# Softmax sums taken from the first pass of the scores by ScalarE, in place of a second product by TensorE

## The reference

```python
x_ln = layernorm(x, ln_g, ln_b)                  # transposed, and read again as (b, 1024, 256)
q = x_flat @ wq + bq
o = gelu(depthwise_conv7x7(q as image, stride 2) + dw_b)
offsets = conv1x1(o, pw_w)                       # 2 numbers at each of 16 x 16 places
interp = bilinear samples of x at refs + tanh(offsets)          # 256 rows of 256 channels
v = interp @ wv + bv ;  k = interp @ wv + bv
qh, kh, vh = heads(q @ mq_w + mq_b), heads(k @ mk_w + mk_b), heads(v @ mv_w + mv_b)
attn = softmax(qh @ kh^T, axis=-1)               # 1024 x 256 for each of 8 heads
z = (attn @ vh, heads joined) @ mo_w + mo_b + x
out = gelu(layernorm(z) @ mlp_w + mlp_b) + z
```

## Time and profile before

| | |
|---|---|
| median of 3 runs | 514.39 us (514.14 to 515.91) |
| profiled execution | 512.36 us |
| span of its trace | 510.6 us |
| TensorE matmul busy | 454.9 us, 89% |
| TensorE weight load busy (overlaps) | 318.8 us, 62% |
| VectorE busy | 286.2 us, 56% |
| ScalarE busy | 211.6 us, 41% |
| GpSimd (POOL) busy | 120.1 us, 24% |
| mean granted TensorE clock | 0.98 |

### The profile page before, as it was taken

One profiled execution on the slowest core, in us unless ns is written; L12 is line 12 of the kernel. 1 busy time (PEld: TensorE's weight loads), 2 busy tenths in 40 slices (PEclk: granted clock), 3 DMA queues, 4 the chain that ended last, 5 costly groups with the idle time before them and its releaser, 6 DMA issues.

```text
span 510.6 us, 9319 instructions
## 1 busy us (share of the span) xinstructions
PE 454.9 (89%) x3743; PEld 318.8 (62%) x3743; DVE 286.2 (56%) x609; ACT 211.6 (41%) x338; POOL 120.1 (24%) x163
## 2 busy tenths in 40 slices
PE   6788979988989999989899999989899897888956
PEld 5657756645567576656686666656767564665735
DVE  4518446846673367667754345567546647625433
ACT  1122212545346045655333336745173664662230
POOL 5420301167003001681002003761030030100000
PEclk9999989989999999999999999999999998999978
DMA  7298866581947930293157801472226200000202
GB/s 211 76 168 171 163 101 126 85 169 65 137 69 99 233 54 3 85 124 64 42 101 103 164 3 46 90 111 27 83 42 86 83 3 2 1 2 2 82 2 83
DMA packets 30489, 42.90 MB, mean 84 GB/s; under 512 B 6075, under 2 KB 21230, under 8 KB 30446
## 3 DMA queue, kind: packets, MB, share of 16 engines
q1 hardware_dynamic: 23598, 34.82, 37.4%
q0 software_dynamic: 3584, 4.50, 3.8%
q10 hardware_dynamic: 3264, 2.99, 2.9%
HBM read 16.16 MB, written 4.19 MB: 40 GB/s over the span
## 4 chain that ended last, share of the span: by engine, by line
PE 57%; DVE 13%; DMA 10%; POOL 7%; issue 5%; ACT 5%; SPq 1%; ACTq 0%; DVEq 0%; POOLq 0%
PE ps_d L759 8%; PE ps_d L884 5%; PE ps_d L861 5%; PE ps_d L961 5%; PE ps_d L747 4%; PE ps_s L808 4%; DMA xa<-in_x_dram 4%; PE ps_v L850 4%; DMA corners<-in_x_dram,row_of 3%; PE ps_v L844 3%; PE ps_t L827 3%; PE ps_d L779 3%; POOL samp L1937 3%; DVE mx L1613 3%; PE ps_d L903 2%
## 5 line engine op out<-in xcount | busy, mean ns | idle before, releaser
L1226 ACT ACTIVATE prob<-ps_t 128x1024 f32<-128x1024 f32 x64 | 65.4, 1021 | 95.8 <-PE ps_t L827 92.2
L1613 DVE TENSOR_REDUCE mx<-ps_s 128x4 f32<-128x1024 f32 x64 | 78.2, 1222 | 24.1 <-PE ps_s L808 23.2
L1909 POOL DMA_DIRECT2D q_st<-mx_t x64 | 34.0, 532 | 244.0 <-ACT mx_t L1218 226.0
L759 PE MATMUL ps_d<-cstack,conv_w 128*32 128x256 f32 x1024 | 59.0, 380 | 3.4 <-issue 1.8
L808 PE MATMUL ps_s<-k_st,q_st 96*128 96x256 f32 x256 | 49.9, 317 | 8.2 <-DVE mx L1613 7.1
L759 PEld LDWEIGHTS ps_d<-cstack,conv_w 128*32 128x32 f32 x1024 | 36.3, 108 | 23.9 <-issue 6.2
L808 PEld LDWEIGHTS ps_s<-k_st,q_st 96*128 96x128 f32 x256 | 35.9, 191 | 20.5 <-DVE mx L1613 12.6
L827 PE MATMUL ps_t<-q_st,k_st 98*128 98x256 f32 x256 | 42.6, 289 | 6.2 <-ACT zt L1285 3.0
L827 PEld LDWEIGHTS ps_t<-q_st,k_st 98*128 98x128 f32 x256 | 35.5, 192 | 8.9 <-issue 5.1
L1627 DVE TENSOR_TENSOR att<-ps_v,rden 128x256 f32<-128x256 f32 x32 | 13.6, 424 | 43.2 <-ACT rden L1237 43.2
L844 PE MATMUL ps_v<-prob,vh 128*32 128x256 f32 x512 | 35.1, 392 | 1.5 <-DVE att L1627 1.5
(11 more groups left out here) (178 smaller groups left out, 744.7 us busy)
## 6 DMA issues: line engine op xcount, KB each, us to landing
q_st<-q_parts SPq DMA_DIRECT2D x42, 256.0 KB, 5.6
xa<-in_x_dram SPq DMA_DIRECT2D x8, 512.0 KB, 9.6
z_all<-in_x_dram SPq DMA_DIRECT2D x8, 512.0 KB, 7.9
out_dram<-z_all SPq DMA_DIRECT2D x8, 512.0 KB, 2.6
cstack<-qpad SPq DMA_DIRECT2D x22, 180.5 KB, 5.7
k_st<-cstack SPq DMA_DIRECT2D x22, 128.0 KB, 4.2
q_st<-z_all SPq DMA_DIRECT2D x6, 256.0 KB, 5.7
cstack<-att SPq DMA_DIRECT2D x6, 180.5 KB, 9.8
```

Of the source, the lines that this page charges most:

```text
L759: ins = pe.matmul(ps[32 * k:32 * k + 32, 0, :], conv_w[:, cb * 4 + k, y, x, :], cstack[:, cb, k, y:y + HG_, x:x + WG_], start=n == 0, stop ...
L1226: drain(act.activation(prob[:, u % 2, 2 * pr:2 * pr + 2].rearrange("p h m s -> p (h m) s"), ps_t[:], ACT.Exp), t_ring, "t", b, u, pr)
L1613: drain(dve.tensor_reduce(mx[:, u % 2, half, :], ps_s[:], AX.X, ALU.max), s_ring, "s", b, u, half)
```

## The change

ScalarE takes the sums of a row over the scores of the first pass. VectorE writes the negated maxima of two heads at a time (`max_neg`). ScalarE then takes, for each of the 4 heads, exp(score - maximum) over `ps_s` in place, with the sum of the row as an additional output (`exp_sums`), and this drains `ps_s`. Then it takes the logarithm of the unit's 16 columns of sums (`log_sums`), and VectorE subtracts the negated maxima from it (`maxima_and_sums`), so that `mx` holds maximum + ln(sum). The rest of the way is the same (turning, copy, rest, two DMAs), but the second pass now gives normalised probabilities. `values_summed`, `denominators` and the product with the reciprocal go; VectorE copies the result (`mixed`).

The order changes too: on TensorE `max_rows` stands behind `values`, and in slot 6 the product "g" and `scores1(m, 0)` stand behind `keys`. ScalarE has `exp_sums` of the first half ahead of `max_out` and the first `exps` (except in slot 0), and `exp_sums` of the second half and `log_sums` ahead of the second `exps`. VectorE has `maxima_and_sums` and `mixed` behind the first half's maxima and ahead of `maxima_lo`. 

```diff
@@ dense_order
+        if in_front(b, s, "off"):
+            order += [("off", n)]
+        if in_front(b, s, "qh1") and b:
+            order += [("qh", n, 1, hg) for hg in range(NHG)]
         if unit_of(b, s, 1):
             order += [("mxt", *unit_of(b, s, 1))]
...
-            order += [("tp", m, 1), ("g", m, 1)] * post
+            order += [("tp", m, 1)] * post
...
             order += [("kh", n)]
+        if s == 6:
+            order += [("g", m, 1)] * post
@@ TensorE
             def max_rows(b, u):
                 ps = open_bank(dense, "mxt", b, u)
-                read_by(s_ring, "s", b, u, 1)
+                pe.wait_ge(shift_done.sem, shift_done.at(b, u + 1))
...
-            def values_summed(b, u):
-                for mt in range(2):
-                    for h in range(HQ):
-                        ins = pe.matmul(ps_v[32 * h:32 * h + 32, 1, :], ones[:], prob[:, u % 2, h, mt, :],
-                                        start=mt == 0, stop=mt == 1)
...
             def slot(b, s):
-                if unit_of(b, s, 1):
-                    max_rows(*unit_of(b, s, 1))
...
                 if unit_of(b, s, 3):
-                    values_mixed(*unit_of(b, s, 3))
+                    values(*unit_of(b, s, 3))
+                if unit_of(b, s, 1):
+                    max_rows(*unit_of(b, s, 1))
...
                 if s == 6 and post:
                     project1(m, "tp", w_tp, 1)
-                    project1(m, "g", w_g, 1)
...
-                if unit_of(b, s, 3):
-                    values_summed(*unit_of(b, s, 3))
...
-                if s == 6 and post:
-                    scores1(m, 0)
                 if in_front(b, s, "kh"):
                     keys(n)
                 if s == 6 and post:
+                    scores1(m, 0)
+                    project1(m, "g", w_g, 1)
                     scores1(m, 1)
@@ ScalarE
-            def denominators(b, u):
...
+            def exp_sums(b, u, half):
+
+                with_exp()
+                for h in range(HQ):
+                    if h % 2 == 0:
+                        act.wait_ge(maxed.sem, maxed.at(b, 4 * u + 2 * half + h // 2 + 1))
+                    ins = act.activation(ps_s[:, h, :], ps_s[:, h, :], ACT.Exp, bias=max_neg[:, u % 2, half, h:h + 1],
+                                         accum_out=sums[:, u % 2, half, h:h + 1])
+                drain(ins, s_ring, "s", b, u, half)
+
+            def log_sums(b, u):
+                k = s_ring.use("s", b, u, 1)
+                act.wait_ge(k.drained, k.done)
+                act.activation(sums[:, u % 2], sums[:, u % 2], ACT.Ln).then_inc(sums_log.sem, 1)
...
             def slot(b, s):
-                if unit_of(b, s, 1):
-                    max_out(*unit_of(b, s, 1))
...
+                if s and cur:
+                    exp_sums(b, s, 0)
+                if s and unit_of(b, s, 1):
+                    max_out(*unit_of(b, s, 1))
                 if unit_of(b, s, 2):
                     exps(*unit_of(b, s, 2), 0)
+                if s == 0 and unit_of(b, s, 1):
+                    max_out(*unit_of(b, s, 1))
...
+                if s == 0 and cur:
+                    exp_sums(b, s, 0)
+                if cur:
+                    exp_sums(b, s, 1)
+                    log_sums(b, s)
                 if unit_of(b, s, 2):
                     exps(*unit_of(b, s, 2), 1)
-                if unit_of(b, s, 3):
-                    denominators(*unit_of(b, s, 3))
@@ VectorE
             def maxima(b, u, half):
                 await_bank(dve, s_ring, "s", b, u, half)
...
-                drain(dve.tensor_reduce(mx[:, u % 2, half, :], ps_s[:], AX.X, ALU.max), s_ring, "s", b, u, half)
+                for pr in range(2):
+                    dve.tensor_reduce(max_neg[:, u % 2, half, 2 * pr:2 * pr + 2], ps_s[:, 2 * pr:2 * pr + 2], AX.X,
+                                      ALU.max, negate=True).then_inc(maxed.sem, 1)
+
+            def maxima_and_sums(b, u):
+
+                dve.wait_ge(sums_log.sem, sums_log.at(b, u + 1))
...
+                dve.tensor_tensor(mx[:, u % 2], sums[:, u % 2], max_neg[:, u % 2], ALU.subtract).then_inc(shift_done.sem, 1)
...
-                drain(dve.tensor_tensor(att[:, hg, c0:c0 + S_], ps_v[:, 0, :], rden[:], ALU.mult), v_ring, "v", b, u)
+                drain(dve.tensor_scalar(att[:, hg, c0:c0 + S_], ps_v[:, 0, :], 1.0, None, ALU.mult), v_ring, "v", b, u)
...
             def slot(b, s):
-                if unit_of(b, s, 1):
-                    maxima_lo(*unit_of(b, s, 1))
...
                 if s and cur:
                     maxima(b, s, 0)
+                if unit_of(b, s, 1):
+                    maxima_and_sums(*unit_of(b, s, 1))
+                if unit_of(b, s, 3):
+                    mixed(*unit_of(b, s, 3))
+                if unit_of(b, s, 1):
+                    maxima_lo(*unit_of(b, s, 1))
```

More of the change, by code:

```diff
@@ L140, in dense_order @@
             order += [("vh", b)]
-        if in_front(b, s, "off"):
-            order += [("off", n)]
         if s == 0:
@@ L162, in dense_order @@
         if s == 6:
-            order += [("tp", m, 1), ("g", m, 1)] * post
+            order += [("tp", m, 1)] * post
         if s == 7 and b == 0:
             order += [("z", b, 0, jp) for jp in range(2)]
-        if in_front(b, s, "qh1"):
+        if in_front(b, s, "qh1") and b == 0:
             order += [("qh", n, 1, hg) for hg in range(NHG)]
@@ L294, in build @@
         vh = sb("vh", [P, 2, C])
+        max_neg = sb("max_neg", [P, 2, 2, HQ])
+        sums = sb("sums", [P, 2, 2, HQ])
         mx = sb("mx", [P, 2, 2, HQ])
@@ L297, in build @@
         prob = sb("prob", [P, 2, HQ, 2, S_])
-        rden = sb("rden", [P, S_])
         att = sb("att", [P, NHG, HW])
@@ L386, in build @@
         max_in = [signal(f"max_in{k}", UNITS, 16) for k in range(2)]
-        den_log = signal("den_log", UNITS)
-        rden_done = signal("rden_done", UNITS)
+        maxed = signal("maxed", 4 * UNITS)
+        sums_log = signal("sums_log", UNITS)
+        shift_done = signal("shift_done", UNITS)
         ln2_stat = signal("ln2_stat", NT)
@@ L831, in values @@
             def values(b, u):
-                values_mixed(b, u)
-                values_summed(b, u)
-            def values_mixed(b, u):
                 hg, _ = unit_at(u)
@@ L843, in values_mixed @@
                         hh = hg * HQ + h
[L844 to L851 removed]
+                        ins = pe.matmul(ps_v[32 * h:32 * h + 32, 0, :], vh[:, mt, hh * HD:(hh + 1) * HD],
+                                        prob[:, u % 2, h, mt, :], start=mt == 0, stop=mt == 1)
                 close_bank(ins, v_ring, "v", b, u)
@@ L1090, in tail @@
             def tail(m):
-                max_rows(m, UNITS - 1)
                 shifted(m, UNITS - 2, 0)
                 values(m, UNITS - 3)
+                max_rows(m, UNITS - 1)
                 shifted(m, UNITS - 2, 1)
@@ L1227, in exps @@
                                      ACT.Exp), t_ring, "t", b, u, pr)
-            def denominators(b, u):
+            def exp_sums(b, u, half):
                 with_exp()
-                await_bank(act, v_ring, "v", b, u)
-                if UNITS * b + u:
-                    k = v_ring.use("v", *divmod(UNITS * b + u - 1, UNITS))
-                    act.wait_ge(k.drained, k.done)
-                act.activation(rden[:], ps_v[:, 1, :], ACT.Ln).then_inc(den_log.sem, 1)
-                act.wait_ge(den_log.sem, den_log.at(b, u + 1))
-                act.activation(rden[:], rden[:], ACT.Exp, scale=-1.0).then_inc(rden_done.sem, 1)
+                for h in range(HQ):
[8 more added lines that the diff above has]
+                act.activation(sums[:, u % 2], sums[:, u % 2], ACT.Ln).then_inc(sums_log.sem, 1)
             def norm_turned(b, cb):
@@ L1343, in tail @@
             def tail(m):
+                exps(m, UNITS - 2, 0)
                 max_out(m, UNITS - 1)
-                exps(m, UNITS - 2, 0)
-                denominators(m, UNITS - 3)
                 exps(m, UNITS - 2, 1)
@@ L1609, in maxima @@
                 await_bank(dve, s_ring, "s", b, u, half)
-                if half == 0 and UNITS * b + u >= 2:
+                for pr in range(2):
[3 more added lines that the diff above has]
+                dve.wait_ge(sums_log.sem, sums_log.at(b, u + 1))
+                if UNITS * b + u >= 2:
                     await_bank(dve, dense, "mxt", *divmod(UNITS * b + u - 2, UNITS))
-                drain(dve.tensor_reduce(mx[:, u % 2, half, :], ps_s[:], AX.X, ALU.max), s_ring, "s", b, u, half)
+                dve.tensor_tensor(mx[:, u % 2], sums[:, u % 2], max_neg[:, u % 2], ALU.subtract).then_inc(shift_done.sem, 1)
             def maxima_lo(b, u):
@@ L1794, in slot @@
                     for_rest.wait(dve)
-                if s == 6 and post:
-                    maxima1(m, 0)
                 if s == 3 and post:
@@ L1807, in slot @@
                     residual_norm(m, 1)
-                if s == 6 and post:
-                    g_rows(m, 1)
```

(2 more changed lines are left out.)

17 lines of the change are left out of this document (6 added, 11 removed).

## The result

The changed kernel takes 603.22 us, median of five runs (600.2 to 609.2), against 514.39 us; the ratio is 1.173, with a 95% interval of 1.168 to 1.179. The forecast was 553 us, at most 587. The sign was right and the size was short by 50 us. Ratios here leave out executions that ran disturbed, so they aren't always the quotient of two medians. The profiled execution took 609.2 us, its span 607.4. It is the longest of the five, 6 us above the median, with a clock of 0.876 where the others had 0.886 to 0.895; a difference of busy or idle time to it can be too large by as much.

The account below looks back on a forecast made before the run. TensorE's queue was taken to set the slots' time; 71 us of new waits less 32 us of removed products gave +39 us on 512.36, 551 us, and 553 as median. Forecast range 530 to 575 us, with rivals B and C 514 to 587.

Parts of the forecast that it names:

- What falls away: TensorE's products with ones go, 1.0 us in each of 32 units, 32 us; ScalarE loses 25.6 us of logarithms and reciprocals.
- What comes, one fill: Score tile held through maxima and four exponentials of 0.46 us each: 3.5 us from fill to fill instead of 2.1.
- Rival C: On ScalarE, the sum's read-out costs a whole small activation, 0.29 us: 587 us in all; chance 0.12.
- Rival B: On ScalarE, four exponentials flow as one long one, hold 2.7 us: 518 us, level with before; chance 0.08.
- 43 holds: About 43 of the score tile's holds stand on the path (12, 11, 10, 10 by batch); 0.09 us per activation is worth 15 us.
- What is queued behind it: Work on ScalarE, VectorE and POOL standing behind the sums, and the moved g projection, makes TensorE wait; slots 5 and 6 +5.6 us.
- shifted in a bare slot: The next slot's shifted products on TensorE wait for ps_t behind ScalarE's sums, logarithm and exps: 0.75 us late.
- (d): On TensorE, the g projection moves from ahead of slot 6's second fill to behind the keys; some 3 us in batches 1 and 2 each.
- Rival A: Follow-on waits are covered by idle ScalarE and TensorE's other work, so only the floors count: 504 us, 2% faster; chance 0.12.
- The sum: Changes in the 64 fills' gaps, by batch +7.3, +12.2, +10.8, +8.8: +39 us, with 71 us of new waits, giving 553 us.
- (a) to (d): Queue waits: ScalarE's copy and exps behind sums, VectorE's maxima_lo behind that copy, POOL's max_row and sampled, the moved g projection.
- gap list: The 64 gaps between score fills, each less 1.0 us, max_rows moved, floored at 3.5 us, queue waits added: +39 us.

Follow-up runs that it names:

- e3: The kernel before without the products with ones, the logarithm and the reciprocal, result not normalised: 500.3 us, ratio 0.967.
- e8: The changed kernel with two plain copies in place of each four exponentials, small logarithm a copy times zero, every wait and order kept: 570.4 us, ratio 1.108.
- e9: The changed order without exponentials, sums and logarithm, with slot 6 in its old order: 517.3 us, ratio 1.005 to the kernel before.
- e6: The kernel before with every score maximum taken twice by VectorE, so the score tile is held longer: 553.7 us, ratio 1.076.
- e10: The kernel before with every score maximum taken twice, plus 49 unread products ahead of the 17 score fills that waited longest: 544.1 us, ratio 1.055.
- e12: The changed kernel with 315 unread products in nearly every TensorE wait over 0.4 us: 587.6 us, ratio 1.139 to the kernel before.
- e13: The changed kernel with the next batch's row scale moved behind the second maxima in slot 4: 600.4 us, ratio 1.160 to the kernel before.
- e5: The changed kernel with 102 unread products ahead of 23 score fills that waited: 602.1 us, ratio 1.172 to the kernel before.
- e2: The changed order without sums or logarithm, VectorE draining the score tile with one maximum, result not normalised: 529.6 us, ratio 1.025 to the kernel before.
- e4: The changed kernel with the score tile split into two banks, each filled and drained for itself: 603.1 us, ratio 1.157 to the kernel before.

## Why the prediction was right or wrong

**What falls away, 32 us.** The work is gone (512 records, ScalarE's rows too), but it is worth 17 us (e3). Idle time grew by 13 us, and busy time fell by 20 us instead of 35, at a clock of 0.949 instead of 0.980.

**What comes, one fill.** Right. 0.45 us for each exponential with its sum (0.46; the 0.09 us for the sum was taken by likeness to another operand, so that it fits is luck in part), a floor of 3.48 us (3.5). Rival C, a read-out as dear as a small activation, falls: the read-out has a record of 204 ns, but it runs within the spacing of 0.45 us. Rival B, four as one, falls with it. That 43 holds are on the path isn't shown: only 22 score fills waited for ScalarE, and e8 gave its 33 us for an expected 32 in part as faster work (25 of the 40 us by which the spans differ).

**What is queued behind it.** Right in part. Slots 0 and 3 of batch 1 came out (table below), `sampled` at 6.1 us, and the value rows of batch 1 open 5.1 us behind slot 2's first fill (5.0). Slots 5 and 6 together are +7.7 and +6.5 us against +5.6. Two of its small sums don't close: slot 2 is given +2.4 us, and its parts add up to 2.2; shifted in a bare slot is called 0.75 us late, and the terms named give 0.55. Neither matters here. (d) is about 10 us of the order's 30 (e9). Rival A, everything covered, falls: the new order alone, without any hold, costs 30 us.

**The sum.** This is the step that failed: "In each I took out 1.0 us, ... put 3.5 us as floor, and added the waits of (a) to (d)". It priced all of TensorE's remaining work at the full clock of the earlier trace rows and added the waits on top. Idle time rose by 72 us, about what the sum had for new waits (71), but the work between them ran at 0.876 instead of 0.98: 482.6 us where 420 was forecast. The prediction named this only as what could push the time above its range, with no term. e6 and e10 show the mechanism in the kernel before, e12 in the changed one, where 15.6 us come back when the clock is held up, with 46.6 us of work added (by the intervals of the ratios, 10 us or more).

Here is batch 1 slot by slot, in us against before, each from first fill to first fill, with the granted clock in brackets:

| slot | forecast | changed | e12 |
|---|---|---|---|
| 0 | +2.3 | +2.2 (1.00) | +2.2 (1.00) |
| 1 | -0.3 | +2.0 (0.76) | -0.7 (1.00) |
| 2 | +2.4 | +4.1 (1.00) | +1.6 (1.00) |
| 3 | -0.2 | -0.2 (1.00) | -0.2 (1.00) |
| 4 | +0.4 | +4.7 (0.94) | +5.7 (0.87) |
| 5, 6 | +5.6 | +7.7 (0.86) | +6.3 (0.90) |
| 7 | +2.0 | +7.8 (0.83) | +5.0 (1.00) |

Where e12 has the full clock, its slots 0 to 3, and slots 0 to 4 of batch 2 too, lie within 0.8 us of the forecast. So the gap list priced these waits well for a TensorE at full clock, which is not the one that the change makes. Slot 7 is the exception: there the second block's shifted scores wait 3.07 us (in e12 2.0 us of fillers and 1.4 us of waiting) for ScalarE's second `exps`, which stands behind the second exp_sums; before, they didn't wait. Before, and then the changed kernel:

```profile
240.87 0.82 PE L930 MATMUL ps_t<-th_st,ph_st 98*128 98x512 f32 x2
```

```profile
286.28 0.70 PE L926 MATMUL ps_t<-th_st,ph_st 98*128 98x512 f32 x2 [3.07 <-ACT prob L1219]
```

The other part of the miss is in the gap list. In e12, with most slots of batches 1 and 2 at full clock, the windows are still +15.7, +20.0, +14.8 and +22.2 us against the forecast's +7.3, +12.2, +10.8 and +8.8. 4.2 us of it is the row scale of slot 4 (e13), and slot 7 has +5.0 and +4.4 us instead of 2.0 each. Most of the rest lies in batches 0 and 3, where there is little work to cover a late queue, and its waits, one by one, were not tried. In all, e12 has 78 us of idle time and 40 us of fillers, 82 us more than the idle time before: at a higher clock the new waits are longer than the 71 us of the sum, not equal to it. So: about 16 of the 50 us are shown to be the clock, and 4 in slot 4 a missed wait. How the other 30 divide stays open, because the two aren't additive: where TensorE runs faster it comes earlier to a wait on ScalarE's chain (e5).

## What to carry to other kernels

When a change adds waits to an engine that was dense, don't add the waits to its work at the old price: take the clock of the new state from rows behind such waits, or measure it by doubling one hold in the old kernel (here 23 us of idle time cost 39 us). Work taken off a dense engine is worth its full time only where the next input is already there; here it was half. And a single tile between three engines is well priced by its floor from fill to fill, which came out to within 1%, while the order of the queues behind it needs every instruction on the waiting engine, those of the next batch too. A time that meets its number isn't yet its reason: in e8 the number for waits alone came out, with much of the gain in faster work.

## What was unexpected of the hardware

The products that are not read made the kernel faster: 587.6 us against 603.2, and 544.1 against 553.7. Waits mostly of 1 to 3 us (the longest 4.9) went with 143 us at 1.2 GHz, and the clock fell even 0.8 us behind the end of a single wait of 1.3 us (at 106.9 us of the changed kernel's trace); idle time went up by 72 us and the mean granted clock went down from 0.98 to 0.876. Over the kernels with the 3231 records of the changed one, the clock goes with the idle time: 0.949 at 49 us (e3), 0.929 at 65 (e2), 0.922 at 92 (e8), 0.883 at 101 (e13), 0.876 at 108; of the two long executions e9 fits (0.928 at 61), and e4 has less (0.876 at 97). The sum of an exponential costs ScalarE little: four of 128x256 with bias and sum come 0.45 us apart, against 0.37 for the nearest row with a bias alone, so some 0.08 us each, although the trace shows a read-out of 0.20 us for each.
